# Moving ScalarE's table load and VectorE's first-norm rows inside a fused cross-attention and feed-forward kernel

## The reference

```
h    = layernorm(x)                                   # the first norm
q    = h @ Wq.T ; k = ctx @ Wk.T ; v = ctx @ Wv.T      # q, k in two halves, 16 heads of 32, 8 kv heads
w    = softmax(q1 k1') - lam * softmax(q2 k2')
a    = w @ v ; a = a * rsqrt(mean(a*a) + eps) * g * (1 - lambda_init)
x    = x + a @ Wo.T
h    = layernorm(layernorm(x))                         # the second norm, with ln1_g, ln1_b behind it
h    = gelu(h @ ternary(w1).T + b1)                    # 2048 wide
out  = x + layernorm(h) @ ternary(w2).T + b2
```

## Time and profile before

| | |
|---|---|
| median of 3 runs | 2459.5 us (2456.2 to 2461.03) |
| the profiled execution's own time | 2460.22 us |
| its span, first to last instruction | 2456.9 us |
| PE busy | 2301.5 us, 94% of the span |
| DVE busy | 1719.6 us, 70% |
| ACT busy | 1339.5 us, 55% |
| POOL busy | 1012.2 us, 41% |
| mean granted TensorE clock | 0.973 of full speed |

### The profile page before, as it was taken

One profiled execution on the slowest core, in us unless ns is written; L12 is line 12 of the kernel. 1 busy time (PEld: TensorE's weight loads), 2 busy tenths in 40 slices (PEclk: granted clock), 3 DMA queues, 4 the chain that ended last, 5 costly groups with the idle time before them and its releaser, 6 DMA issues.

```text
span 2456.9 us, 35564 instructions
## 1 busy us (share of the span) xinstructions
PE 2301.5 (94%) x13663; PEld 1082.5 (44%) x13663; DVE 1719.6 (70%) x2714; ACT 1339.5 (55%) x1943; POOL 1012.2 (41%) x823
## 2 busy tenths in 40 slices
PE   8488999999999999999999999999999999999978
PEld 5243444535344453535444353534445353544433
DVE  3865858678585868768586776858586785857563
ACT  3325555546555555556555555655555465555544
POOL 0220543617153452716345271625436172534517
PEclk9688999999999999999999999999999999999989
DMA  6220203021130302111030202103030211202000
GB/s 256 74 77 11 69 15 89 13 69 26 37 84 15 90 15 68 25 60 44 23 97 15 78 15 69 36 23 82 15 101 19 65 27 33 72 15 74 15 22 17
DMA packets 105643, 125.85 MB, mean 51 GB/s; under 512 B 22496, under 2 KB 74268, under 8 KB 104964
## 3 DMA queue, kind: packets, MB, share of 16 engines
q1 hardware_dynamic: 105476, 123.60, 17.4%
HBM read 51.80 MB, written 20.36 MB: 29 GB/s over the span
## 4 chain that ended last, share of the span: by engine, by line
PE 69%; DVE 19%; issue 3%; ACT 3%; POOL 3%; DMA 2%; SPq 1%; POOLq 0%; ACTq 0%; DVEq 0%
PE ps L1325 16%; PE ps L1337 9%; PE ps L1347 7%; PE ps L1272 5%; PE ps L1225 5%; PE ps L1250 4%; PE ps L1173 4%; PE ps L1279 4%; PE ps L1174 3%; PE ps L1175 3%; DVE attn_raw L928 2%; DVE arena L987 2%; DVE arena L876 2%; DVE arena L890 2%; PE ps L1255 2%
## 5 line engine op out<-in xcount | busy, mean ns | idle before, releaser
L526 POOL TENSOR_TENSOR attn_raw<-attn_raw 128x512 f32<-128x512 f32 x448 | 580.2, 1314 | 146.5 <-ACT attn_raw L685 138.7
L1325 PE MATMUL ps<-rows,w1T 128*128 128x512 f16 x2048 | 485.5, 380 | 24.1 <-DVE rows L982 24.1
L890 DVE TENSOR_REDUCE arena<-ps 128x3 f32<-128x462 f32 (+1 forms) x704 | 413.8, 619 | 96.5 <-PE ps L1225 95.4
L494 POOL TENSOR_TENSOR q<-q 128x512 f16<-128x512 f32 x128 | 155.9, 1222 | 695.3 <-ACT q L631 678.5
L680 ACT ACTIVATE attn_raw<-ps,vec_cols,wstep 128x512 f32<-128x512 f32 x256 | 198.6, 776 | 267.0 <-PE ps L1325 265.2
L987 DVE SCALAR_TENSOR_TENSOR arena<-attn_raw,vec_cols,arena 128x512 f16<-128x512 f32 x256 | 233.1, 911 | 84.7 <-ACT arena L683 83.2
L1325 PEld LDWEIGHTS ps<-rows,w1T 128*128 128x128 f16 x2048 | 191.0, 97 | 220.7 <-DVE rows L982 37.2
L651 ACT ACTIVATE arena<-ps 128x1024 f32<-128x1024 f32 x128 | 131.6, 1028 | 266.6 <-PE ps L1250 266.6
L1347 PE MATMUL ps<-w2T,arena 128*128 128x512 f16 x1088 | 271.1, 379 | 0.0
L910 DVE SCALAR_TENSOR_TENSOR p<-arena,p 128x512 f16<-128x512 f32 x128 | 88.1, 689 | 254.4 <-ACT p L655 254.4
L1225 PE MATMUL ps<-k_att,stack_raw 96*128 96x154 f16 x2048 | 223.2, 234 | 23.1 <-DVE arena L890 21.6
(11 more groups left out here) (164 smaller groups left out, 3436.5 us busy)
## 6 DMA issues: line engine op xcount, KB each, us to landing
stack_raw<-q SPq DMA_DIRECT2D x768, 64.0 KB, 2.0
arena<-in_x SPq DMA_DIRECT2D x16, 1024.0 KB, 6.2
arena<-in_x SPq DMA_DIRECT2D x64, 256.0 KB, 2.6
out<-arena SPq DMA_DIRECT2D x64, 256.0 KB, 2.0
arena<-in_L_ffn_w SPq DMA_DIRECT2D x8, 1024.0 KB, 10.5
stack_raw<-in_L_xattn_Wq SPq DMA_DIRECT2D x8, 256.0 KB, 10.8
k_att<-k_store SPq DMA_DIRECT2D x4, 490.0 KB
k_store<-attn_raw SPq DMA_DIRECT2D x12, 160.0 KB
```

Source lines behind the costliest of these rows:

```text
L526: ins = pool.tensor_tensor(acc[:, e, :], acc[:, e, :], src[:, j % NG, :], ALU.add)
L890: dve.tensor_reduce(negmax[:, tt, u0:u1], ps[:, row_bank(c, tb), 0:(u1 - u0) * S].rearrange("p (u s) -> p u s", s=S), AX.X, ALU.max, negat ...
L1325: ins = pe.matmul(ps[:, B_H + j % 2, :], w1T[:, k, j * P:(j + 1) * P], rows16[:, e, k, :], start=(k == 0 and e == 0), stop=(k == KD - 1 an ...
```

## The change

It does two things. On ScalarE, the load of Gelu's table now stands ahead of the copies of queries 4 to 6 and no longer behind them. On VectorE, ln1_rows(i+2) no longer runs between mid_rows and h_lo: its first two instructions stand behind gelu_lo(0), its last two behind gelu_lo(1).

```
+LN1_ROWS_AT = {0: (0, 1), 1: (2, 3)}
...
+                load_table(ACT.Gelu)
                 if ahead:
                     for n in range(QATT, QEARLY):
                         q_hi(i + 1, n)
-                load_table(ACT.Gelu)
                 h_hi(i)
...
-            def ln1_rows(c):
+            def ln1_rows(c, tts=range(TT)):
 
                 wait(dve, s_rstd1, c, 1, 1)
-                for tt in range(TT):
+                for tt in tts:
...
                 mid_rows(i)
-                if ahead2:
-                    ln1_rows(i + 2)
                 h_lo(i)
                 for j in range(JH):
                     beside = maxima_beside(j) if ahead else []
                     for tb in beside[:2]:
                         row_max(i + 1, tb)
                     gelu_lo(i, j)
+                    if ahead2 and j in LN1_ROWS_AT:
+                        ln1_rows(i + 2, LN1_ROWS_AT[j])
                     for tb in beside[2:]:
                         row_max(i + 1, tb)
```

## The result

| | before | with the change |
|---|---|---|
| median | 2460.01 us (2456.2 to 2461.03, 4 runs) | 2486.3 us (2484.98 to 2487.41, 4 runs) |
| span of the profiled execution | 2456.9 us | 2482.7 us |
| mean granted TensorE clock | 0.973 | 0.967 |

The ratio is 1.011, 95% interval 1.0092 to 1.0127: the change costs 26 us, the forecast was 24. The page of the changed kernel shows TensorE's wait ahead of hidden(0) gone in all blocks but the last (2.2 us are left) and the one ahead of row_scores more than doubled (the last two columns are the idle time before the group and what ended it; before they were 24.1 and 23.1).

A forecast was written before the change was run, and what follows sets the result against it. Bound: TensorE's waits for VectorE, slowed by turns with GpSimd, up to its last wait in each block. 21.0 + 1.0 - 0.7 + 3.5 = +24.8 on 2460.22 gives 2485, median 2484 us; range 2466 to 2502.

The forecast's parts named there:

- Parts 1 and 2: Table load into ScalarE's idle time, ln1_rows out from ahead of h_lo: hidden(0) 1.74 us earlier; block 14 gains 0.70.
- part 3: ln1_rows behind gelu_lo(0) and (1): turns with GpSimd delay the maxima, TensorE past its last wait 1.50 us later per block.
- Rival B: gelu_lo(3) comes just before GpSimd's sixth addition: +0.8 us per block, about 2472 us; chance 0.08.
- The term for the clock: TensorE's clock falls behind the 3.0 us wait in about half of 14 blocks, 0.5 us net each: +3.5 us.
- rival C: TensorE's clock falls in every block, its time all on the path: 24 us for the clock, 2505 us; chance 0.08.
- 21 + 1 + 3.5 - 0.7: Sum: 14 blocks at 1.50 us, block 3's smaller gain, the clock's falls, block 14's gain: +24.8 us.
- Rival A: VectorE absorbs the rows in idle at j = 0 and 1, no turns lost: 2434 us, chance 0.08; draw 2459, 0.10.
- The figure of the Trainium skill: GpSimd blocked until VectorE's end plus about 115 ns: three added turns cost 0.26 us more each, 11 us in all (2495).

The follow-up runs named there:

- e7: The change with ten more matmuls on TensorE behind hidden(3) in blocks 0 to 13, filling most of its 2.8 us wait: 2468.96 us, ratio 1.004 to before.
- e8b: The change with GpSimd's additions for j = 1 to 4 cut to 8 of 512 columns: 2427.27 us; the kernel before with the same cut: 2439.27 us.
- e3: The change with all four ln1_rows behind gelu_lo(0), none behind gelu_lo(1): 2442.2 us, ratio 0.9932 to before.
- e5: The change with one ln1_rows ahead of gelu_lo(j) for each j = 5 to 8: 2436.36 us, ratio 0.991 to before.
- e6: The change with two ln1_rows between mid_rows and h_lo and two right behind h_lo: 2433.64 us, ratio 0.9897 to before.
- e10: The change with one ln1_rows behind gelu_lo(j) for each j = 5 to 8: 2510.11 us, ratio 1.0205 to before.

## Why the prediction was right, and where it was not

- **Parts 1 and 2 held within 0.04 us.** The load is hidden, h_hi follows the transposes, hidden(0) starts 0.22 behind the last matmul of query 7 (1122.30 in the frame of before), and block 14 is 0.73 us shorter (0.70 forecast).
- **The walk of part 3 held up to gelu_lo(2).** In the frame of before gelu_lo(1) ends at 1130.11 (30.19 forecast), row 2 at 1131.52 (31.59), row 3 at 1132.92 (32.99), maximum 3 releases TensorE at 1133.53 (33.59), gelu_lo(2) ends at 1134.67 (34.66).
- **The step that failed, in part 3: "gelu_lo(3) asked for at 34.58 + 1.18 = 35.76, and, as before, just after G's sixth".** The 1.18 is the length of two maxima from start to last end; the next instruction starts 1.09 behind their start (1149.33 to 1150.42). Before, gelu_lo(3) stood 1.17 behind its maxima because it waited for ScalarE's high half too, and that was ready here. So it was asked for at 35.69, and GpSimd's sixth (1150.49, 35.76 in the frame) came 0.07 after it. Rival B's turn was the real one, at its price: 0.73 us a block and not 1.50. That is 14 x 0.77 = 10.8 us less than forecast.
- **The term for the clock was mis-sized the other way.** The sum had 0.5 us in half of the blocks, 3.5 us, since 0.85 us of the loss was to be absorbed by waits. With gelu_lo(3) free there was no such wait left to absorb it: in the seven blocks with a fall and no batch change near (1, 2, 4, 5, 9, 10, 12) it cost 2.27 to 2.74 less 0.73, 1.5 to 2.0 us, and it came in 11 of 14. Filling the wait (e7) measures 17.3 us in all: rival C's price for a fall (1.7 us) was about right, its fall in every block was not. Why the clock holds in blocks 6, 8 and 13, whose wait is as long, and falls in block 11 behind 1.87 us, the runs do not settle; the forecast's reason, a wait longer than those before, does not separate them. So the block period that was to show the forecast, 142.2 to 142.7 us, is met by none of the blocks away from a batch change: they are 141.4 or 142.96 to 143.4 us long.
- **So the total is better than its parts.** 14 x 0.73 + 17 - 0.7 is 26.5 us against 25.8 between the spans; the forecast's 21 + 1 + 3.5 - 0.7 was 24.8. The two errors cancel, so that 24 came so near to 26 is luck; the one wrong turn is behind the first and behind part of the second, how often the clock falls was a guess. The cause and the place were right and are shown: e8b takes the turns away and the sign of the change flips, e3, e5 and e6 move the rows out of the turns and all or most of the early start is kept.
- **Rival A** needed gelu_lo(1) and rows 2 and 3 to be held for less than 1.25 us together; they were held for 0.90 + 0.95 + 0.94 = 2.8. **The figure of the Trainium skill** for the handover (SBUF — State Buffer, "A bandwidth-pool intuition that's wrong": 115 ns behind VectorE's end, measured there on a DMA whose descriptors GpSimd writes) would have made the change dearer. The trace does not agree with it for these additions: they again end 1.12 us behind VectorE's end (1147.65 to 1148.77), as in the earlier trace rows, with 1.26 us as their length alone.

## What to carry to other kernels

An engine's idle time is not one pool. With the table load in its new place, the four instructions give 2458 us when all stand ahead of h_lo, 2434 when they stand around it, 2442 all behind gelu_lo(0), 2436 one by one ahead of gelu_lo(5) to (8), and 2486 where the change put them, in the stretch where VectorE's time sets the pace. Where VectorE and GpSimd both work from SBUF, walk them together and ask who starts first; one place in the list decided here between 2436 and 2510 us. And look at both halves of a combined edit in every pairing: the table's move is worth nothing or about 10 us depending on where the rows stand, and a forecast of the sum can be right by errors that cancel.

## What the runs showed of the hardware that I had not expected

- Ten useless matmuls in a wait of 2.8 us made the kernel 17 us faster (e7 against the change), by keeping the clock at its upper level.
- A wait of 1.87 us was followed by a fall of the clock (block 11 of the changed kernel), and waits of 2.81 to 2.82 us in blocks 6, 8 and 13 were not.
- Between VectorE and GpSimd a waiting instruction is served before the other engine's next one. In the changed kernel gelu_lo(1) waited through GpSimd's first addition, and the second, issued at 1144.24, ended at 1145.96, 1.12 behind gelu_lo(1)'s end at 1144.84: turns are exact enough for a walk on paper to stay within 0.1 us over four of them. Who comes first cannot be read off the starts when they are this close: VectorE's record began 0.07 us before GpSimd's at gelu_lo(3) of the changed kernel and VectorE went first, and 0.03 us before it at gelu_lo(6) of e10 and GpSimd went first.
- In this stretch a VectorE instruction that is not held by another engine's semaphore begins 0.07 to 0.09 us before the one ahead of it ends; taking lengths in place of start-to-start distances is what cost the forecast its turn.
